# Attention scores in units of 32 queries of four heads in place of 64 queries of two

## What is computed

```python
qkv = q @ w_qkv.T
scores = jnp.einsum('bskgd,btkd->bkgst', qh, kh) * scale
scores = jnp.where(causal, scores, jnp.finfo(scores.dtype).min)
probs = jax.nn.softmax(scores, axis=-1)
attn = jnp.einsum('bkgst,btkd->bskgd', probs, vh)
x = x + _layernorm(attn.reshape(...) @ w_dense.T)
x = x + _layernorm(ffn(_layernorm(x)))      # silu(g) * u, 1792 wide, block-quantised inputs
```

## Time and profile before

| | |
|---|---|
| median of 3 runs | 1243.08 us (1241.71 to 1245.66) |
| profiled execution | 1241.49 us |
| its span, first to last instruction | 1239.7 us |
| granted TensorE clock | 0.997 of full speed |
| busy: PE, DVE, POOL, ACT | 1208.3, 789.4, 695.9, 608.8 us |

### The profile page before, as it was taken

The page is one execution under the profiler, slowest core; times in us unless marked ns, Lnnn a source line. Parts: engine busy times, 40 slices in busy tenths (PEclk is TensorE's granted clock), DMA queues, the critical chain, the costliest instruction groups (busy, mean ns, idle before and its releaser), DMA issues.

```text
span 1239.7 us, 18158 instructions
## 1 busy us (share of the span) xinstructions
PE 1208.3 (97%) x6188; PEld 1001.6 (81%) x6188; DVE 789.4 (64%) x1945; ACT 608.8 (49%) x1365; POOL 695.9 (56%) x822
## 2 busy tenths in 40 slices
PE   9999999999999999999999999999998799999996
PEld 7788888888888888888888888888877578888885
DVE  4644544466676666666766666767778765655568
ACT  6433243256666666656666666657667521111111
POOL 7745455434735645536535536527556687776645
PEclk9999999999999999999999999999999999999998
DMA  6534553330120020020120210200400101011101
GB/s 215 147 151 170 195 196 137 136 136 19 35 85 27 26 85 27 26 94 26 35 77 26 81 39 20 93 26 26 145 18 2 51 30 63 14 49 51 51 0 68
DMA packets 59457, 89.74 MB, mean 72 GB/s; under 512 B 3440, under 2 KB 44400, under 8 KB 56048
## 3 DMA queue, kind: packets, MB, share of 16 engines
q1 hardware_dynamic: 59376, 88.70, 20.7%
HBM read 61.43 MB, written 27.26 MB: 72 GB/s over the span
## 4 chain that ended last, share of the span: by engine, by line
PE 85%; DVE 5%; ACT 4%; POOL 3%; issue 1%; DMA 1%; POOLq 0%; ACTq 0%; DVEq 0%; SPq 0%
PE psS L1113 24%; PE psOY L1225 16%; PE psOY L1113 14%; PE psOY L1240 11%; PE psT L1113 10%; PE psT L1209 8%; DVE pT_lo L830 2%; ACT pT_hi L684 1%; PE psS L1261 1%; ACT probs_short L689 1%; ACT qT_hi L678 1%; DVE oT_lo L830 1%; DVE st L833 1%; ACT oT_hi L794 1%; DVE probs_long L886 0%
## 5 line engine op out<-in xcount | busy, mean ns | idle before, releaser
L466 POOL TENSOR_SCALAR probs_long<-probs_long,rsum 128x960 f32<-128x960 f32 (+7 forms) x128 | 121.0, 945 | 259.3 <-DVE rsum L894 258.9
L830 DVE TENSOR_TENSOR pT_lo<-psT,pT_hi 128x512 fp32r<-128x512 f32 (+3 forms) x384 | 211.7, 553 | 80.4 <-ACT pT_hi L684 77.0
L684 ACT CAST pT_hi<-psT 128x512 fp32r<-128x512 f32 (+3 forms) x384 | 182.2, 476 | 69.0 <-PE psT L1209 67.6
L1113 PE MATMUL psS<-kT_hi,qT_hi 128*128 128x256 f32 (+4 forms) x384 | 149.5, 389 | 0.0
L1209 PE MATMUL psT<-ident,probs_long 128*128 128x128 f32 x832 | 135.4, 276 | 9.3 <-DVE pT_lo L830 8.8
L689 ACT ACTIVATE probs_long<-probs_long,negmax 128x960 f32<-128x960 f32 (+7 forms) x128 | 123.8, 967 | 37.9 <-DVE negmax L886 37.9
L1209 PEld LDWEIGHTS psT<-ident,probs_long 128*128 128x128 f32 x832 | 100.7, 140 | 51.0 <-DVE pT_lo L830 33.8
L1113 PE MATMUL psS<-kT_hi,qT_lo 128*128 128x256 f32 (+4 forms) x384 | 128.9, 336 | 0.0
L1113 PE MATMUL psS<-kT_lo,qT_hi 128*128 128x256 f32 (+4 forms) x384 | 128.5, 335 | 0.0
L886 DVE CUSTOM_DVE_ANT_0 probs_long<-psS,mask 128x960 f32<-128x960 f32 (+7 forms) x128 | 126.0, 985 | 2.9 <-PE psS L1113 1.1
L1225 PE MATMUL psOY<-pT_hi,v_hi 128*128 128x512 f32 x288 | 118.2, 410 | 1.3 <-DVE pT_lo L830 1.3
(11 more groups left out here) (150 smaller groups left out, 2965.4 us busy)
## 6 DMA issues: line engine op xcount, KB each, us to landing
q_raw<-q_scr SPq DMA_DIRECT2D x64, 256.0 KB, 2.9
raw<-in_w_qk SPq DMA_DIRECT2D x10, 1024.0 KB, 5.8
q_scr<-cB SPq DMA_DIRECT2D x16, 512.0 KB, 2.6
q_scr<-cA SPq DMA_DIRECT2D x16, 512.0 KB, 2.6
raw_wd<-in_w_dense SPq DMA_DIRECT2D x8, 1024.0 KB, 7.7
raw_up<-in_w_up SPq DMA_DIRECT2D x7, 1024.0 KB, 4.8
v_scr<-vout SPq DMA_DIRECT2D x16, 256.0 KB, 2.4
kT_lo<-k_scr SPq DMA_DIRECT2D x8, 512.0 KB, 4.3
```

The costliest lines, as they stand in the source:

```text
L466: nc.gpsimd.tensor_scalar(row, row, rsum[:, h:h + 1], 1.0, ALU.mult, ALU.mult).then_inc(p_ready, 1)
L684: nc.scalar.copy(dst, src).then_inc(t_hi, 1)
L830: return nc.vector.tensor_tensor(dst, source, hi.bitcast(F32), ALU.subtract)
L1113: last = nc.tensor.matmul(dst, a, b, start=(start and k == 0), stop=(stop and k == len(terms) - 1), skip_group_check=resumed)
```

## The change

A unit is now 32 queries of all four heads: unit u holds queries 32 u to 32 u + 31. Its keys end at i * 128 + 32 (u + 1), so the four units of a block need 32, 64, 96 and 128 keys past i * 128, in place of 64, 128, 64 and 128: 64 columns fewer in a block, 16 in a unit on average. The mask's slanted part is 32 columns wide; three memsets in place of two zero the ends of each buffer. The access patterns that order queries by unit change with it: `qT_hi` and `qT_lo` are written, and `qT_hi` is read by POOL, four elements (16 bytes) apart instead of two, in runs of 32 queries; `psO` is read four elements apart, and `oT_hi` and `oT_lo` are written in runs of 32.

```diff
--- before.py
+++ after.py
@@ -66,7 +66,7 @@
 
 
 
-    HALF = P // 2
+    SPAN = P // HG
 
     def step_items(t):
         s, g, items, following, two = t % NT, t // NT, [], t < T - 1, p_banks(t) == 2
@@ -124,7 +124,7 @@
         return t * HG + h + 1
 
     def keys_of(t, u):
-        return ORDER[t % NT] * P + HALF * (u % 2 + 1)
+        return ORDER[t % NT] * P + SPAN * (u + 1)
 
     def score_offset(n):
 
@@ -261,15 +261,15 @@
                 return [t[:, piece * BANK:(piece + 1) * BANK] for t in kT[e]]
             return [t[:, (piece - 2) * TPB:(piece - 1) * TPB, :] for t in v[e]]
 
-        def in_pairs(tile):
-
-            return tile[:].rearrange("p (m q b) -> p m b q", m=HG // 2, b=2)
+        def by_unit(tile):
+
+            return tile[:].rearrange("p (u q b) -> p u b q", u=HG, b=HG)
 
         def by_head(tile):
-            return tile[:].rearrange("p (m b q) -> p m b q", m=HG // 2, b=2)
-
-        def by_pair(tile):
-            return tile[:].rearrange("p (m b) q -> p m b q", b=2)
+            return tile[:].rearrange("p (b u q) -> p u b q", u=HG, b=HG)
+
+        def raw_by_unit(tile):
+            return tile[:].rearrange("p b (u q) -> p u b q", u=HG)
 
         def turned(item):
             _, t, b, h = item
@@ -447,8 +447,8 @@
 
             def restore_q(t):
                 pool.wait_ge(q_hi, t + 1)
-                hi, lo = (in_pairs(u) for u in qT[t % 3])
-                low(lo, by_pair(q_raw[t % 2]), hi).then_inc(q_lo, 1)
+                hi, lo = (by_unit(u) for u in qT[t % 3])
+                low(lo, raw_by_unit(q_raw[t % 2]), hi).then_inc(q_lo, 1)
 
             def split_dense(g, h):
                 if h == 0:
@@ -543,8 +543,8 @@
                     values_weight(1, i - 2)
             nc.gpsimd.memset(mask[:], 0.0).then_inc(const_ready, 1)
             pool.wait_ge(const_ready, 4)
-            nc.gpsimd.affine_select(out=mask[:, S - HALF:S], in_=mask[:, S - HALF:S], compare_op=ALU.is_ge, fill=NEG,
-                                    base=0, pattern=[[-2, HALF]], channel_multiplier=1).then_inc(const_ready, 1)
+            nc.gpsimd.affine_select(out=mask[:, S - SPAN:S], in_=mask[:, S - SPAN:S], compare_op=ALU.is_ge, fill=NEG,
+                                    base=0, pattern=[[-HG, SPAN]], channel_multiplier=1).then_inc(const_ready, 1)
             weight_sums(0)
             weight_blocks(0)
 
@@ -566,13 +566,13 @@
                         split_dense(0, h)
 
             pool.wait_ge(p_full, 7 * (QUADS - 2))
-            for u in (0, 2):
-                nc.gpsimd.memset(probs_short[:, u, BANK - HALF:BANK], 0.0).then_inc(const_ready, 1)
+            for u in range(HG - 1):
+                nc.gpsimd.memset(probs_short[:, u, BANK - SPAN * (HG - 1 - u):BANK], 0.0).then_inc(const_ready, 1)
             for h in range(HG):
                 norm_head(0, h)
             pool.wait_ge(p_full, 7 * QUADS)
-            for u in (0, 2):
-                nc.gpsimd.memset(probs_long[:, u, S - HALF:S], 0.0).then_inc(const_ready, 1)
+            for u in range(HG - 1):
+                nc.gpsimd.memset(probs_long[:, u, S - SPAN * (HG - 1 - u):S], 0.0).then_inc(const_ready, 1)
 
             for kind, *args in ATTENTION:
                 if kind == "E":
@@ -675,7 +675,7 @@
                 act.wait_ge(q_in[t % 2], 16 * (t // 2 + 1))
                 if t >= 3:
                     act.wait_ge(s_full, (t - 2) * HG)
-                nc.scalar.copy(in_pairs(qT[t % 3][0]), by_pair(q_raw[t % 2])).then_inc(q_hi, 1)
+                nc.scalar.copy(by_unit(qT[t % 3][0]), raw_by_unit(q_raw[t % 2])).then_inc(q_hi, 1)
 
             def hi_of_turn(item):
                 dst = turned(item)[0]
@@ -791,7 +791,7 @@
                     restore_q(*args)
                 elif kind == "O":
                     act.wait_ge(o_full, args[0] + 1)
-                    nc.scalar.copy(by_head(oT[0]), in_pairs(psO)).then_inc(o_hi, 1)
+                    nc.scalar.copy(by_head(oT[0]), by_unit(psO)).then_inc(o_hi, 1)
                 elif kind in ("center_y", "norm_y", "center_x1", "norm_x1"):
                     norms(kind, *args)
 
@@ -1041,7 +1041,7 @@
                     add_projection(*args)
                 elif kind == "O":
                     dve.wait_ge(o_hi, args[0] + 1)
-                    lo_part(by_head(oT[1]), in_pairs(psO), by_head(oT[0])).then_inc(o_done, 1)
+                    lo_part(by_head(oT[1]), by_unit(psO), by_head(oT[0])).then_inc(o_done, 1)
                 elif kind == "stat_y":
                     output_statistics(*args)
                 elif kind == "residual":
```

## The result

| | before | changed |
|---|---|---|
| median of 6 runs | 1243.77 us (1241.71 to 1245.66) | 1251.24 us (1249.16 to 1255.44) |
| ratio, 95% interval | | 1.0066 (1.0046 to 1.0086) |
| profiled execution | 1241.49 us | 1255.44 us |

The changed kernel is 0.66% slower, where 1250.5 us was forecast.

The account below looks back on a forecast made before the run. PE, 97% busy, bounds the kernel, with the queries' cast on its path in long steps. 1241.5 - 2.75 (scores) + 10.2 (slower cast) = 1249.0, or 1250.5 us as a median; range 1236 to 1263.

Parts of the forecast that it names:

- The mechanism: ACT's `qT_hi` cast, writing four elements apart, delays PE's turn P(t, 1, 1) in 31 long steps by 0.33 us each: +10.2 us.
- the 1024-column row: Measured cast of 1024 columns, 1057 ns, taken as the high end for `qT_hi` at a step of four: +0.40 us.
- the two exponentials ahead of the cast: Exponentials ahead of `qT_hi` on PE's path, 32 and 64 columns shorter: 0.084 us for both, 0.07 taken per long step.
- The savings: Score passes on PE, 64 columns fewer in six blocks: 4.1 us, of which 2.75 us in short steps were counted.
- the first rival: The stepped `qT_hi` write is free, near 0.66 us: -4.1 of scores, -1.1 in blocks 5 and 6, 1238 us; 28%.
- the reading of the kernel before: In every long step the queries' cast is on PE's path; PE loses 0.36 and 0.21 us in blocks 5 and 6.
- What I costed at nothing: POOL's `qT_lo`, hidden (at most +1.3 us), and the `psO` reads of `oT_hi` and `oT_lo`: each taken as 0.
- the rival with the PSUM reads: `oT_hi` and `oT_lo` together up to 0.98 us longer, delaying output shares: 14 us more, 1265 us; 14%.

Follow-up runs that it names:

- pattern_alone: Changed kernel with the key ends of before (64, 128, 64, 128 past the block), all access patterns as changed: 1258.28 us, ratio 1.0136.
- act4_pool2: Changed kernel, but POOL's subtraction `qT_lo` uses the step of two on all operands, ACT's cast keeps four: 1251.39 us, ratio 1.0069.
- the first four experiments: keys_alone, pattern_alone, act4_pool2 and act2_pool4, compared with runs of the kernel before on the same chip, median 1242.45 us.
- keys_alone: Changed kernel with its shorter keys, but `qT_hi` and `qT_lo` written two elements apart as before: 1237.98 us, ratio 0.9965.
- act2_pool4: Changed kernel, but ACT's cast `qT_hi` uses the step of two, POOL's subtraction keeps four: 1238.08 us, ratio 0.9963.
- before_moved: Kernel before, with restore_q moved in long steps from ahead of turn P(t,0,3) to behind turn P(t,1,3): 1239.96 us, ratio 0.9985.
- heads_apart: Changed kernel, but each unit laid out head after head, 32 neighbouring queries each, mask made per head: 1237.03 us, ratio 0.9958.

## Why the prediction was right, point by point

**The mechanism held; that the size agrees so well is partly luck.** The cast grew, by 0.466 us where I took 0.40 from the 1024-column row; at each long step's turn PE waits 0.33 us longer (1326 / 4), and I had forecast 0.33. Two errors of equal size cancel: the cast is 66 ns longer, and 0.13 us of it is absorbed, not 0.07. pattern_alone splits that: 0.045 is absorbed with the old key ends (462 - 417), so there was a little room that I hadn't seen, and the new key ends give (384 - 291 + 662 - 604 + 788 - 683 + 483 - 397) / 4 = 86 ns, near the upper end, 0.084, of what I worked out for the two exponentials ahead of the cast. That it is these rows alone is not shown.

**The savings** were mis-sized. I let 2.75 us of 4.1 count beside a slow cast, since what PE saves on the scores of blocks 2 and 3, in long steps, would be lost ahead of the turn. It isn't. PE's waits at the turns grow by 1326 ns a group, but the four long steps by only 1156, and the 170 between them match the 2 x 86 ns saved on blocks 2 and 3. The four short steps shrink by 341 ns, which matches the 4 x 86 of the other blocks. So all 4.1 us are saved. This fits pattern_alone too: against it the key ends are worth 1258.28 - 1251.39 (act4_pool2, which ran with it) = 6.9 us, and 4.1 + 31 x 0.086 = 6.8; with the 2.75 it would be 5.4.

By the step lengths the change costs 8 x 0.815 = 6.5 us, where I had 10.2 - 2.75 = 7.5; the medians are 7.5 apart, with an interval of 5.7 to 10.7. So the near-exact hit has about 1 us in it that is not in the steps' work. The half-clock stretches are of that size: runs with the same mean clock of 0.996 took 1249.16 and 1249.95 us with the change and 1242.35 to 1243.68 without (six of the twelve beside the first four experiments), a difference of 6.6 us between their means.

With a cheap cast the key ends are worth 4.5 us, where the first rival had 4.1 + 1.1. So that rival, 1238 us, was the right price of a free write: keys_alone and act2_pool4 measured it.

**The step that failed is the reading of the kernel before.** I wrote that PE loses 0.36 and 0.21 us in blocks 5 and 6 because "in every long step the cast of the queries is on PE's path". It was only just on it. Taking the cast away altogether (before_moved) gives back 73 and 39 ns in the first seven groups; only in the last is it 0.54 us in each. The rest is the round trip of a turn through its bank. I had seen a chain without a gap on ACT, and not checked that ACT's next cast couldn't have begun earlier for another reason: the transposes that it reads had only just ended (669.75 + 0.60 = 670.35, and it began at 670.46). The forecast survived since the cast grew far beyond this edge: of 0.466 us, 0.33 count.

**What I costed at nothing.** `qT_lo` grew by 0.25 us and is hidden (act4_pool2, act2_pool4); `oT_hi` and `oT_lo` did not change (586 and 690 ns), so the rival with the PSUM reads has no mechanism: steps of four in PSUM cost no more than steps of two. The Trainium skill's rule for GpSimd's reads ("GPSIMD Engine Reference", Performance pitfalls for Q7 kernels) has the right sign, and 1566 against 1312 ns is 19%, not 50, with only one of two inputs stepped.

**What I didn't price** is the clock. Stretches at half clock, some 1.6 us each, widen the runs of the slower kernels and lift their medians by up to 2.5 us (an estimate: the mean clocks above, 0.994 and 0.996, differ by 0.002, and that of 1250 us); what brings them on stays open.

## What to carry to other kernels

Before taking a finer unit for the columns that it saves, look at how the rearranging access patterns change: here a step from 8 to 16 bytes on one small cast, 64 times, cost 13.3 us against a saving of 4.5, and laying the same elements out in runs kept the saving whole. When two engines hand a buffer to and fro, a gapless chain in the trace has two possible causes; ask of each link whether its input was there earlier. What stands ahead of the last turn in such a loop can be moved to where its engine waits, as long as its user is far enough behind: here that gave the kernel before 1.5 us, gave heads_apart nothing that can be told, where most turns were at their floor already, and cost 0.27 us a group where the scores then waited for the queries.

## What the runs showed of the hardware

ACT moves a 128x512 float32 cast in SBUF in 610 ns in runs of 32 neighbours, 658 at a step of 8 bytes or in pairs, 1122 at 16 bytes, 1184 at 32 bytes, and 1120 when it is the reads that are 512 bytes apart. POOL's two-input subtraction went from 1312 to 1566 ns with one input and the output at 16 bytes. ACT and DVE read PSUM at steps of 8 and 16 bytes at one price (586 and 586 ns, 691 and 690).
